# Layer 2 attention: scores contracted over the 32 rows of a batch, 512 columns a product, two batches in alternation

## The reference, cut to what matters

```python
def _L2_attn_ref(x, wq, wk, wv, wo, lora_A_q, ...):
    ...
    q = proj(wq, lora_A_q, lora_B_q).reshape(B, S, N_HEADS, HEAD_DIM)   # 16, 256, 4, 8
    ...
    q = _rope(q, cos, sin).transpose(0, 2, 1, 3)
    k = _rope(k, cos, sin).transpose(0, 2, 1, 3)
    ...
    scores = jnp.einsum('bhqd,bhkd->bhqk', q, k) * INV_SQRT_HD
    causal = jnp.triu(jnp.ones((S, S), dtype=bool), k=1)
    scores = jnp.where(causal[None, None], -jnp.inf, scores)
    attn = jax.nn.softmax(scores, axis=-1)
    out = jnp.einsum('bhqk,bhkd->bhqd', attn, v)
    return out.transpose(0, 2, 1, 3).reshape(B, S, DIM) @ wo.T
```

## Time and profile before

| what | value |
|---|---|
| median of 3 runs (lowest, highest) | 774.87 us (772.77, 777.02) |
| the profiled execution: its span | 775.8 us |
| TensorE matmul busy | 566.2 us, 73% |
| VectorE busy | 340.6 us, 44% |
| ScalarE busy | 336.1 us, 43% |
| mean granted TensorE clock | 0.763 of 2.4 GHz |

### The profile page before, as it was taken

How to read it: one execution, slowest core, us unless ns; L and a number is a source line. 1 busy time by engine, 2 the same in 40 slices (tenths; PEclk the granted TensorE clock), 3 DMA queues, 4 the chain that set the end, 5 groups by cost and what they waited for, 6 DMA issues and landing times. The chain is left out here.

```text
span 775.8 us, 10987 instructions
## 1 busy us (share of the span) xinstructions
PE 566.2 (73%) x4080; PEld 324.7 (42%) x4081; DVE 340.6 (44%) x734; ACT 336.1 (43%) x1095; POOL 0.2 (0%) x4
## 2 busy tenths in 40 slices
PE   6665566567877999986566666665899998995463
PEld 5322222235645766664333333333455544551321
DVE  2170000049757788875200000006887546776233
ACT  2233333337737677772333333334544465442121
POOL 0000000000000000000000000000000000000000
PEclk9755555559997999997555555558999999997577
DMA  4000000000000000000000000004000000000000
GB/s 166 1 1 1 1 0 1 1 0 1 3 0 1 2 1 2 2 1 1 1 1 1 0 1 1 0 1 108 1 2 1 1 1 1 2 1 0 8 5 27
DMA packets 4954, 6.73 MB, mean 9 GB/s; under 512 B 1186, under 2 KB 4642, under 8 KB 4772
## 3 DMA queue, kind: packets, MB, share of 16 engines
q1 hardware_dynamic: 4900, 6.01, 2.5%
HBM read 3.38 MB, written 0.52 MB: 5 GB/s over the span
## 5 line engine op out<-in xcount | busy, mean ns | idle before, releaser
L303 PE MATMUL ps<-arena,wsb 16*16 16x16 f32 (+1 forms) x1024 | 131.5, 206 | 111.1 <-ACT arena L321 111.1
L321 ACT ACTIVATE arena<-ps 16x16 f32<-16x16 f32 (+1 forms) x512 | 96.3, 188 | 199.3 <-PE ps L303 199.3
L303 PEld LDWEIGHTS ps<-arena,wsb 16*16 16x16 f32 (+1 forms) x1024 | 76.4, 118 | 196.2 <-ACT arena L321 191.7
L327 DVE TENSOR_TENSOR X<-X,ps 128x128 f32<-128x128 f32 x16 | 4.6, 288 | 206.6 <-PE ps L288 206.6
L965 ACT ACTIVATE arena<-ps 128x512 f32<-128x512 f32 x96 | 56.6, 597 | 62.0 <-PE ps L726 60.7
L1267 DVE TENSOR_TENSOR arena<-arena,ps 128x512 f32<-128x512 f32 x96 | 64.0, 685 | 41.2 <-ACT arena L965 24.9
L744 PE MATMUL ps<-arena 128*32 128x128 f32 x768 | 60.3, 279 | 7.3 <-DVE arena L1267 7.3
L889 ACT ACTIVATE arena<-ps,arena 128x128 f32<-128x128 f32 (+1 forms) x128 | 52.4, 418 | 29.9 <-DVE arena L1140 29.8
L744 PEld LDWEIGHTS ps<-arena 128*32 128x32 f32 x768 | 34.8, 109 | 41.9 <-DVE arena L1267 22.6
L1139 DVE TENSOR_REDUCE arena<-ps 128x2 f32<-128x512 f32 (+1 forms) x48 | 33.0, 688 | 18.6 <-PE ps L569 11.1
L586 PE MATMUL ps<-wsb,arena 128*128 128x128 f32 x192 | 30.4, 282 | 11.6 <-DVE arena L1148 11.5
(11 more groups left out here) (231 smaller groups left out, 805.8 us busy)
## 6 DMA issues: line engine op xcount, KB each, us to landing
arena<-xn SPq DMA_DIRECT2D x16, 128.0 KB, 2.5
wsb<-weights SPq DMA_DIRECT2D x1, 1916.5 KB, 8.8
wsb<-weights SPq DMA_DIRECT2D x1, 549.5 KB, 4.8
X<-x SPq DMA_DIRECT2D x1, 512.0 KB, 3.9
out<-X SPq DMA_DIRECT2D x1, 512.0 KB, 3.0
csb<-consts SPq DMA_DIRECT2D x1, 160.0 KB, 8.8
arena<-w SPq DMA_DIRECT2D x2, 64.0 KB
arena<-b SPq DMA_DIRECT2D x4, 0.5 KB
```

What stands on the lines that cost most here:

```text
L303: nc.tensor.matmul(step_columns(k, rows, r), w_state, states[0:rows, :, :, t].rearrange("p g j -> p (g j)"), start=False, stop=True, skip_ ...
L321: nc.scalar.activation(states[0:rows, :, :, t + 1].rearrange("p g j -> p (g j)"), step_columns(t // STEP_BANK, rows, t % STEP_BANK), func) ...
```

## The change

Three things are changed together.

1. **Keys.** `kz` has 4 copies, one per head, instead of 16: copy h keeps the 8 rows of head h in every batch group. ScalarE writes one of them, VectorE three, all before the loop. TensorE waits for all of them before its first score product.
2. **Scores.** A product takes only the 32 partitions of its batch group as contraction rows, for the queries and the keys. The four (or two) heads of a unit are one product of 512 columns. The mask products stay as they are.
3. **Order.** Units go by pairs of batches: part 0 of one, part 0 of the other, then parts 1, then parts 2. A batch's last units are now neighbours, and so are the two pv and the two out products of a pair. The distances (pv three iterations after a batch's last unit, out five) stay.

```diff
+        def l2_unit(u):
+            pair, n = u // 6, u % 6
+            return 2 * pair + n % 2, n // 2
...
+        def l2_batch_ending(u):
+            return 2 * (u // 6) + u % 2 if u >= 0 and u % 6 in (4, 5) and u < UNITS else None
...
+            pe.wait_ge(s["L2 keys"], 2)
             for u in range(UNITS + 5):
                 if u < UNITS:
-                    b, part = u // 3, u % 3
+                    b, part = l2_unit(u)
                     j, g = b // G, b % G
-                    if b < G and part == 0:
-                        pe.wait_ge(s["L2 keys"] if g % 2 else s["L2 keys scalar"], g // 2 + 1)
+                    rows = slice(C * g, C * g + C)
...
-                        for h in range(HEADS):
-                            mm = nc.tensor.matmul(bank[:, h * P:(h + 1) * P], q[:, j, 0:P], kz[:, g * HEADS + h, j, 0:P],
-                                                  start=False, stop=(h == HEADS - 1))
+                        mm = nc.tensor.matmul(bank, q[rows, j, 0:P], kz[rows, :, j, 0:P], start=False, stop=True)
                     else:
-                        for h in range(2):
-                            nc.tensor.matmul(bank[:, h * T:(h + 1) * T], q[:, j, P:T],
-                                                  kz[:, g * HEADS + 2 * (part - 1) + h, j, :], start=(h == 0), stop=False)
+                        nc.tensor.matmul(bank, q[rows, j, P:T], kz[rows, 2 * (part - 1):2 * part, j, :], start=True, stop=False)
...
-                if u >= 5 and (u - 5) % 3 == 0 and (u - 5) // 3 < B:
-                    b = (u - 5) // 3
+                b = l2_batch_ending(u - 3)
+                if b is not None:
...
-            keys_scalar(0)
+            nc.scalar.activation(kz[:, 3, :, :].rearrange("p j t -> p (j t)"), qk[:, 1, :], ACT.Copy,
+                                 scale=W("head_rows")[:, 3:4]).then_inc(s["L2 keys"], 1)
...
+            for h in range(3):
+                ins = nc.vector.tensor_scalar(kz[:, h, :, :].rearrange("p j t -> p (j t)"), qk[:, 1, :],
+                                              W("head_rows")[:, h:h + 1], None, ALU.mult)
+            ins.then_inc(s["L2 keys"], 1)
```

More of the change, by code:

```diff
@@ L62 @@
     ("L2_A_q", P), ("L2_A_k", P), ("L2_A_v", P), ("L2_B_qT", P), ("L2_B_kT", P), ("L2_B_vT", P),
-    ("cos", T), ("sin", T), ("head_mask", G * HEADS), ("L2_wo_by_head", C),
+    ("cos", T), ("sin", T), ("head_rows", HEADS), ("L2_wo_by_head", C),
     ("F_WT", P), ("F_VT", P), ("F_gamma", 1), ("F_beta", 1), ("avg_g", P),
@@ L184, in hybrid_block @@
         qrs = at(N)
-        kz = at(G * HEADS, J, T)
+        kz = at(HEADS, J, T)
         by_query = at(3, HALF)
@@ L190, in hybrid_block, with l2_last_unit, l2_slot @@
         fst = sb("fst", [P, 8])
+        def l2_unit(u):
+            pair, n = u // 6, u % 6
+            return 2 * pair + n % 2, n // 2
+        def l2_last_unit(b):
+            return 6 * (b // 2) + 4 + b % 2
+        def l2_slot(b, part):
+            return 2 * part + b % 2
+        def l2_batch_ending(u):
+            return 2 * (u // 6) + u % 2 if u >= 0 and u % 6 in (4, 5) and u < UNITS else None
         at = Arena()
@@ L554, in _ @@
             q = qk[:, 0, :].rearrange("p (j t) -> p j t", j=J)
+            pe.wait_ge(s["L2 keys"], 2)
             for u in range(UNITS + 5):
                 if u < UNITS:
-                    b, part = u // 3, u % 3
+                    b, part = l2_unit(u)
                     j, g = b // G, b % G
-                    if b < G and part == 0:
-                        pe.wait_ge(s["L2 keys"] if g % 2 else s["L2 keys scalar"], g // 2 + 1)
+                    rows = slice(C * g, C * g + C)
                     if u >= 3:
                         pe.wait_ge(s["L2 exp"], u - 2)
-                    bank = ps[:, part, :]
+                    bank = ps[:, u % 3, :]
                     if part == 0:
@@ L588, in _ @@
                     mm.then_inc(s["L2 turned"], 1)
-                if u >= 5 and (u - 5) % 3 == 0 and (u - 5) // 3 < B:
-                    b = (u - 5) // 3
+                b = l2_batch_ending(u - 3)
+                if b is not None:
                     j, g = b // G, b % G
-                    pe.wait_ge(s["L2 turned saved"], 3 * (b + 1))
+                    pe.wait_ge(s["L2 turned saved"], l2_last_unit(b) + 1)
                     if b >= 2:
@@ L600, in _ @@
                             mm = nc.tensor.matmul(ps[C * h:C * h + C, 6 + b % 2, qt * P:(qt + 1) * P],
-                                                  vt[:, j * TT + kt, C * g:C * g + C], prob6[:, (3 * b + part) % 6, c0:c0 + P],
+                                                  vt[:, j * TT + kt, C * g:C * g + C], prob6[:, l2_slot(b, part), c0:c0 + P],
                                                   start=(kt == 0), stop=(kt == qt))
                     mm.then_inc(s["L2 pv"], 1)
-                if u >= 7 and (u - 7) % 3 == 0:
-                    b = (u - 7) // 3
+                b = l2_batch_ending(u - 5)
+                if b is not None:
                     pe.wait_ge(s["L2 attended"], b + 1)
@@ L879, in _ @@
             for u in range(UNITS + 2):
-                if u == 1:
-                    keys_scalar(2)
                 if u < UNITS:
-                    heads, width = (HEADS, P) if u % 3 == 0 else (2, T)
+                    heads, width = (HEADS, P) if l2_unit(u)[1] == 0 else (2, T)
                     act.wait_ge(s["L2 minus max"], u + 1)
@@ L897, in _ @@
                     if v >= 6:
-                        act.wait_ge(s["L2 pv"], v // 3 - 1)
+                        act.wait_ge(s["L2 pv"], l2_unit(v - 6)[0] + 1)
                     nc.scalar.activation(prob6[:, v % 6, :], ps[:, 3 + v % 3, :], ACT.Copy).then_inc(s["L2 turned saved"], 1)
@@ L1119, in _ @@
                 dve.wait_ge(s["L2 rotated"], i + 1)
[L1121 to L1126, removed]
+            for h in range(3):
+                ins = nc.vector.tensor_scalar(kz[:, h, :, :].rearrange("p j t -> p (j t)"), qk[:, 1, :],
+                                              W("head_rows")[:, h:h + 1], None, ALU.mult)
+            ins.then_inc(s["L2 keys"], 1)
             for u in range(UNITS + 6):
[L1129 to L1132, removed]
                 if u < UNITS:
-                    heads = HEADS if u % 3 == 0 else 2
+                    heads = HEADS if l2_unit(u)[1] == 0 else 2
                     dve.wait_ge(s["L2 scores"], u + 1)
@@ L1143, in _ @@
                     v = u - 1
-                    heads = HEADS if v % 3 == 0 else 2
+                    heads = HEADS if l2_unit(v)[1] == 0 else 2
                     dve.wait_ge(s["L2 exp"], v + 1)
@@ L1149, in _ @@
                                             .to_broadcast([P, heads, HALF // heads]), ALU.mult).then_inc(s["L2 probabilities"], 1)
-                if u >= 6 and (u - 6) % 3 == 0 and (u - 6) // 3 < B:
-                    b = (u - 6) // 3
+                b = l2_batch_ending(u - 4)
+                if b is not None:
                     dve.wait_ge(s["L2 pv"], b + 1)
@@ L1156, in _ @@
                     nc.vector.tensor_copy(oat[:, (b % G) * T:(b % G + 1) * T], ps[:, 6 + b % 2, 0:T]).then_inc(s["L2 attended"], 1)
-                if u >= 8 and (u - 8) % 3 == 0:
-                    b = (u - 8) // 3
+                b = l2_batch_ending(u - 6)
+                if b is not None:
                     dve.wait_ge(s["L2 out"], b + 1)
@@ L1417, in _pack @@
     put("group_mask", np.repeat(np.eye(G), C, axis=0))
-    put("head_mask", np.repeat(np.eye(G * HEADS), HD, axis=0))
+    put("head_rows", np.tile(np.repeat(np.eye(HEADS), HD, axis=0), (G, 1)))
     by_head = np.zeros((HEADS, C, C), np.float32)
```

## The result

The changed kernel takes 828.92 us in the median of 4 runs (822.12 to 837.5), the one before 775.94. The ratio is 1.0606, 95% interval 1.055 to 1.0662. The runs fall in two groups, 822 and 836 us; the ratio is made from the first, and the profiled run is one of the second (835.33 us), so its stage is read against its own span. The mean granted clock of the whole run is 0.708 and 0.715 in the first group and 0.702 and 0.690 in the second, against 0.763 before, so both groups lost clock.

A forecast was written before the change was run, and what follows sets the result against it. TensorE bounds the stage, with one wait for VectorE. Loop 246.0 + 7 x 14.4 = 346.9, plus an end of 6.7, puts the next norm at 353.6, 2.4 later: 774.9 + 2.4 = 777.3 us, range 768 to 785.

The forecast's parts named there:

- the clock: In the changed stage: lower level for the first 3.4 us as before, then 1.00 from 238 on.
- Rival 3: Clock falls in iterations 0 and 1 of each pair: 12 us, 789; near 842 if low throughout; chance 0.13.
- the timetable of a pair: Two batches in the new order take 14.4 us instead of 13.20, with waits of 0.4, 0.5 and 0.7.
- the borders: Changes of shape around the 32-row score products cost TensorE 0.20 to 0.23 us, four times per pair.
- rival 1: A change of rows at the score products is free: a pair 13.9 us, the whole 773.2; chance 0.2.
- Rival 2: The new order's waits for ScalarE's copy or VectorE's product don't come: minus 1.4 us per pair, 767.5; chance 0.12.
- the start: Key copies leave the loop, so the third batch starts at 246.0, not 251.90: minus 5.9 us.
- what follows the stage: Everything from the next norm on is unchanged and depends only on its start, 353.6 instead of 351.20.
- the working for out's columns: Out's 512 columns in the loop take 0.43 us, at the transposes' rate of 256 in 0.11.
- rival 4: Score products of different batch groups overlap: up to 2.6 us per pair, 18 over all; chance 0.05 including the rest.

The follow-up runs named there:

- filler: Changed kernel plus one 128-row product of zero weights per unit: 799.81 us; with the first six units also over 128 rows: 785.28 us.
- masked-queries run: Against the kernel before: 4 key copies, 4 query copies masked by batch group, 512-column products over 128 rows, old order; 771.97 us, repeated 773.69 us.

## Why the prediction was wrong, point by point

- **Failed: the clock.** The step was "the clock will be at its lower level for the first 3.4 us as it was", and the whole loop at 1.00 after that. I carried the granted clock over from a trace whose products all had 128 rows (or 32 output columns). The runs show that it depends on the rows: low until 265 with 32 rows, and at 0.54 for 238 to 258 with 64, where 128 rows have 1.00. Everything in the sum that stands behind this step was a time at full clock: the stage was to take 119.8 us (233.8 to 353.6) and took 173.1, with the clock at 0.50 in 136 of them.
- **Rival 3 named it and was mis-sized.** It was put at the waits of iterations 0 and 1, at 12 us, and the sentence on "a quarter of the rows" came last, with 842 as the price of a full loss. Measured were 822 to 837, that is a loss for part of the stage. The waits by themselves cost no clock (128 rows, 1.0001); with 32 rows the order does matter (one of four against ten of ten).
- **Right: the timetable of a pair.** 14.30 for 14.4, with its waits; 13.93 for 13.9 without the borders of rows; 15.2 with a filler. **Right: the borders**, a little smaller: 14.30 less 13.93 is 0.37 per pair, forecast 0.5. A change of rows is not free, so rival 1 was wrong (13.9 was its number for 32 rows). Rival 2 was wrong too: the waits came.
- **Right, but hidden: the start.** The third batch was to start at 246.0. With 128 rows in the first pair it does (245.67). In the changed kernel it starts at 251.69, since those 17 us ran at half rate.
- **Wrong in small: what follows the stage.** It was said to depend on the stage's end alone. In the masked-queries run 3.4 of the 7.5 us saved are lost again behind it. Also the working for out's columns doesn't come out as written (512 at 256 in 0.11 us are 0.22, not 0.43). The 0.43 itself fits, as half of the 0.86 of a 512-column product, so nothing behind it moves.
- **The uncertainty.** For 0.13 on rival 3 I had "waits of 0.5 never brought one" as evidence against, which spoke to the waits and not to the rows. There was no row in the trace of a 32-row product at full clock, and the bound of that cost had to include the clock: 842 belonged into the range. At the other end the range of 768 to 785 was said to take in most of rival 2, whose own number, 767.5, lies below it.

## What to carry to other kernels

Before cutting the contraction of a product to fewer rows, ask what will hold TensorE's clock: zeros that are multiplied along cost no time at equal clock, and they may be what keeps the clock up. A cost that is taken from rows at full clock holds only as long as the clock does, so where a change alters how many rows of the array its products use, the price of a whole stage at half rate is one end of the range. Parts of a change that come together (fewer copies, fewer rows, another order) can be worth having apart. Here fewer copies gain 0.5 to 0.7% with full rows and the old order, the pairs take that back, and the 32 rows cost the 6%.

## What the runs showed that I had not expected

**Work added, time saved.** 48 products more made the kernel 22 us faster. The Trainium skill (TensorE: Matmul & The Clock Gate, Why this matters for your kernels) says that a single product with a contraction of 32 takes the same time as one with 128. At full clock the rows agree: the 32-row product of 512 columns takes 1.06 to the next mask (276.73 to 277.79) and the 128-row one 0.96 (277.67 to 278.63), the difference being the border. But the clock was not equal: from 289 to 338 it was 0.50 with 32 rows and 1.00 with 128.

**Two products of different batch groups at once.** At the start of the loop, where no transposes stand between them, unit 1 (L581) and unit 2 (L583) of the changed kernel start together, at the lower clock:

```profile
237.38 1.22 PE L581 MATMUL ps<-arena 32*128 32x512 f32 x1
237.39 1.22 PE L583 MATMUL ps<-arena 32*128 32x512 f32 x1
238.40 1.06 PE L581 MATMUL ps<-arena 32*128 32x512 f32 x1
238.41 1.06 PE L583 MATMUL ps<-arena 32*128 32x512 f32 x1
239.40 0.39 PE L584 MATMUL ps<-csb 128*128 128x256 bf16 x1
```

They have different rows and different banks. Both are through by the next mask, 2.02 us after their start, where one alone takes 2.00 at this clock (332.81 to 334.81). That is the overlap of rival 4; it occurs once, in the only place where nothing stands between two scores. With 128 rows the same two products follow each other.

**What stays open.** The clock can fall without any idle time, here in the old-order run with 32 rows:

```profile
325.52:335.00 9.48, 9.48 (x60) 4.22 (x56) 7.49 (x20) 6.47 (x25) 0.00 (x0) 1.00 0.00 1
336.00:342.00 6.00, 6.00 (x36) 2.68 (x34) 3.40 (x9) 3.37 (x13) 0.00 (x0) 0.50 0.01 3
```

TensorE is busy throughout. What in the pair order loses the clock, and what ends a low stretch after 31 us in one run and 44 in another, these runs don't tell.
